# Score tasks and a probability task placed between the key blocks of the weighted sums, and three exponents ahead of ScalarE's copy of the heads

## The reference

```python
x = x + attn(layernorm(x))       # q, k, v = x @ Wq, x @ Wk, x @ Wv; s = (q * scale) @ k^T, causal
                                 # p = softmax(s); o = p @ v; attn = o @ Wo + bo
x = x + moe(layernorm(x))        # top 2 of 8 experts by softmax of x @ gate_w^T
                                 # relu(x @ w1[e] + b1[e]) @ w2[e] + b2[e], weighted by the probabilities
```

## Time and profile before

| | us |
|---|---|
| median of 3 runs | 533.49 (533.24 to 535.54) |
| span of the profiled execution | 527.7 |
| TensorE busy | 469.7 (89%) |
| VectorE busy | 413.1 (78%) |
| ScalarE busy | 358.9 (68%) |
| GpSimd busy | 286.6 (54%) |

### The profile page before, as it was taken

How to read it: one execution, slowest core, us unless ns; L and a number is a source line. 1 busy time by engine, 2 the same in 40 slices (tenths; PEclk the granted TensorE clock), 3 DMA queues, 4 the chain that set the end, 5 groups by cost and what they waited for, 6 DMA issues and landing times.

```text
span 527.7 us, 14330 instructions
## 1 busy us (share of the span) xinstructions
PE 469.7 (89%) x4121; PEld 328.0 (62%) x4121; DVE 413.1 (78%) x1519; ACT 358.9 (68%) x782; POOL 286.6 (54%) x579
## 2 busy tenths in 40 slices
PE   3788999999999999999999999989788789999981
PEld 1545656556555545546555545459688679999980
DVE  6898878988988888888888897875556555557875
ACT  7576877777867867876866857875456457777750
POOL 5603544535755766657657565725456555545542
PEclk9879999999999999999999999999999899999997
DMA  7434232132233233233333326722222322235653
GB/s 225 134 93 129 56 118 91 56 118 88 67 120 108 70 108 110 76 101 97 102 95 98 106 76 175 209 65 63 56 63 69 85 77 74 71 79 180 182 172 101
DMA packets 49454, 54.92 MB, mean 104 GB/s; under 512 B 6564, under 2 KB 41554, under 8 KB 49377
## 3 DMA queue, kind: packets, MB, share of 16 engines
q1 hardware_dynamic: 44736, 45.18, 29.5%
q0 software_dynamic: 4320, 8.47, 4.7%
q10 hardware_dynamic: 320, 0.36, 0.2%
HBM read 34.96 MB, written 17.90 MB: 100 GB/s over the span
## 4 chain that ended last, share of the span: by engine, by line
PE 50%; DVE 28%; ACT 7%; issue 7%; DMA 4%; another core or an unknown queue 3%; ACTq 1%; SPq 0%; POOL 0%; DVEq 0%; POOLq 0%
PE psO L1035 12%; DVE psS L1349 10%; PE psT L1197 7%; DVE maxs L1352 7%; PE psS L998 7%; PE psM L1208 5%; PE psO L1208 5%; PE psT L1011 3%; PE psS L1197 2%; ACT PT L811 2%; DMA xs_t<-sorted_x 2%; PE psS L1187 2%; DVE maxs L1349 1%; DVE xn L1278 1%
## 5 line engine op out<-in xcount | busy, mean ns | idle before, releaser
L811 ACT ACTIVATE PT<-psT 128x512 f32<-128x512 f32 x320 | 172.5, 594 | 67.6 <-PE psO L1035 45.0
L1349 DVE CUSTOM_DVE_ANT_0 psS<-mask_row,psS 128x512 f32<-128x512 bf16 (+1 forms) x232 | 142.8, 624 | 33.6 <-PE psS L998 29.3
L998 PE MATMUL psS<-Ks,Qs 96*128 96x128 bf16 (+3 forms) x512 | 132.9, 308 | 9.5 <-DVE maxs L1352 7.3
L598 POOL TENSOR_SCALAR_AFFINE_SELECT PT<-PT 128x512 f32<-128x512 f32 x124 | 76.8, 635 | 96.0 <-ACT PT L811 94.8
L1011 PE MATMUL psT<-Qs,Ks 108*128 108x384 bf16 (+3 forms) x512 | 109.9, 299 | 4.2 <-ACT PT L811 3.0
L695 POOL DMA_INDIRECT token_y<-Qs,y_row x71 | 70.8, 997 | 74.6 <-DVE Qs L1750 39.0
L998 PEld LDWEIGHTS psS<-Ks,Qs 96*128 96x128 bf16 x512 | 50.4, 99 | 53.5 <-DVE maxs L1352 26.4
L629 POOL DMA_INDIRECT sorted_x<-xn,place x64 | 64.3, 1005 | 27.6 <-issue 16.5
L1352 DVE TENSOR_REDUCE maxs<-psS 128x2 f32<-128x512 f32 (+3 forms) x120 | 75.7, 669 | 1.8 <-PE psS L1001 1.4
L1035 PE MATMUL psO<-PT,Vs 128*32 128x512 f32 (+3 forms) x1024 | 75.8, 436 | 0.3 <-DVE x_all L1375 0.3
L1011 PEld LDWEIGHTS psT<-Qs,Ks 108*128 108x128 bf16 x512 | 43.5, 97 | 32.8 <-ACT PT L811 12.9
(11 more groups left out here) (260 smaller groups left out, 741.1 us busy)
## 6 DMA issues: line engine op xcount, KB each, us to landing
Qs<-q_parts SPq DMA_DIRECT2D x96, 96.0 KB
Ks<-k_parts SPq DMA_DIRECT2D x95, 96.0 KB
xs_t<-sorted_x SPq DMA_DIRECT2D x71, 65.0 KB
w_sb<-in_L_ffn_w SPq DMA_DIRECT2D x16, 256.0 KB
k_parts<-kparts SPq DMA_DIRECT2D x8, 384.0 KB, 2.6
q_parts<-qparts SPq DMA_DIRECT2D x8, 384.0 KB, 3.6
x_all<-in_L_attn_x SPq DMA_DIRECT2D x8, 256.0 KB, 4.7
v_all<-token_y SPq DMA_DIRECT2D x4, 512.0 KB, 4.4
```

The source lines that it names most:

```text
L598: pool.affine_select(out=square, in_=square, compare_op=ALU.is_ge, fill=0.0, base=0, pattern=[[0, GH], [1, P]], channel_multiplier=-1).the ...
L811: act.activation(PT[:, n * T:(n + 1) * T], psT[:, bank, :], ACT.Exp).then_inc(prob_done[bank], 1)
L998: last = pe.matmul(psS[:, bank, c0:c0 + n], Qs[0:QK_ROWS, g, h, j * P:n], Ks[0:QK_ROWS, g, h, 0:n], start=True, stop=alone)
L1349: dve.tensor_tensor_reduce(src, mask_row[:, (CH - 1 - j) * P:], src, 1.0, NEG, ALU.add, ALU.max, maxs[:, par, j, h:h + 1]).then_inc(scores ...
```

## The change

On TensorE the four key blocks of the weighted sums no longer stand together. Score task 3 and probability task 2 stand between block 0 and block 1, score task 4 between block 3 and block 2, and `turn_shift` moves behind block 2. No instruction is added or removed. On ScalarE the exponent of probability task 2 moves from behind the copies of the heads and of the maxima to in front of them.

```diff
@@ ScalarE, step
                 exps(s, 0)
                 exps(s, 1)
+                exps(s, 2)
                 if not (first and g == 0):
                     copy_heads(s - 1, (g + 3) % GROUPS)
...
                 for n in range(2, NPROB):
-                    exps(s, n)
+                    if n > 2:
+                        exps(s, n)
@@ TensorE, step
-                weighed(*KEY_BLOCKS)
-
-                if nxt:
-                    turn_shift(s + 1, b + (g + 1) // GROUPS, (g + 1) % GROUPS)
+                weighed(KEY_BLOCKS[0])
                 sc(3)
                 if before:
                     probs(s, b, g, 2)
-                sc(4, 5)
+                weighed(*KEY_BLOCKS[1:3])
+                sc(4)
+                weighed(KEY_BLOCKS[3])
+                if nxt:
+                    turn_shift(s + 1, b + (g + 1) // GROUPS, (g + 1) % GROUPS)
+                sc(5)
                 probs(s, b, g, 3)
```

## The result

The changed kernel takes **547.36 us** (median of 4 runs, 546.71 to 547.92) against 533.8 us for the kernel before (4 runs on the same chip, 533.24 to 535.54): 1.0264 times as long, interval 1.0235 to 1.0293. The prediction was 540.3 with a range up to 546. The direction was right, the size half of what came.

A forecast was written before the change was run, and what follows sets the result against it. TensorE was taken as the fuller engine, VectorE also near its limit mid-attention. Early steps 3.4, five batch entries 3.2 and last steps 0.2 gave 6.8 us on 533.5: 540.3 us, range 529 to 546.

The forecast's parts named there:

- The bound: Attention steps: TensorE is the fuller engine, busy 42.1 of 43 us early and 37.9 of 40 in the middle.
- The border: TensorE, where narrow and full weights meet: 0.10 us each, four more borders, 0.40 us a step.
- The handover: Block 2 to ScalarE's copy to `turn_heads`: loses its cover, 0.2 us wait; with borders, score task 6 0.62 later.
- The copy of the maxima: ScalarE, behind the copy of the heads: done at 4.49 us after the sums' start, just hidden behind `turn_heads`.
- The exponent in front of the copy: ScalarE's third exponent: ends by 2.8 us, before the copy can begin at 3.43, so it costs nothing.
- VectorE's hole: VectorE's 1.16 us wait, outside the chain: filling it keeps 0.1; rival that it pays: 526 us, chance 0.17.
- how much later score task 6 comes: TensorE, per step: 0.62 us early; in the middle 0.24 (g = 1), 4.11 to 4.55 (g = 2), 0.3 (g = 3), 0.62 (g = 0).
- Where waits take it up: TensorE's waits for VectorE: five early steps pay 0.3 us; middle g = 3 pays nothing, g = 0 and 2 pay 0.2.
- The handover hit by scatters: Rival: GpSimd's scatters delay the copy with g = 0 and 2, 5 us more, 545 us; 0.13 shared with dearer borders.
- The last steps: The last three attention steps: hardly any score tasks, 0.2 us in all.
- The base: The 6.8 us, reckoned on a span of 527.7, was added to the median of 533.5 us.

The follow-up runs named there:

- the pair with extra matmuls: Kernel before plus two unread 16-column matmuls per step between key blocks: 128-column weights 521.61 us (1.0292), 32-column weights 508.97 us (1.0029).
- first and second set: Two sets of follow-up runs, each on one chip together with the kernel before, which took 507.39 and 507.19 us there.
- Putting a task back as cover: Changed kernel with score task 6 ahead of `turn_heads`: 519.47 us, 1.025 times the kernel before.
- a late copy alone, with no border: Kernel before with only ScalarE's new order, the third exponent in front of the copies, and TensorE's old order: 526.0 us, 1.0374 times before.
- the second set: Changed kernel run again, beside parts of the change, on a chip where the kernel before takes 507.19 us: 524.04 us, 1.0337 times before.
- the third set: Kernel before (533.37 us) with edits to ScalarE's and GpSimd's lists; with the scatter issued in the next step, 536.87 us, 1.0066 times before.

## Why the prediction had the sign right and the size wrong

**The bound: right for three groups of four.** TensorE was the fuller engine, and 68% of the chain after runs through it. Steps with g = 0 hang in part on VectorE, as below.

**The border: right, a little small.** Forecast 0.10 each, 0.40 a step. The changed kernel's step shows 0.13 + 0.09 + 0.14 + 0.10 = 0.46, and the pair with extra matmuls 0.44. The pair also shows that it hangs on the width of the weights, not on cutting the run. The Trainium skill, TensorEngine Tiling (Array Packing), section Tiling Modes, says that a change of the mode "drains the TensorE". These runs agree that a change of the width costs, 0.11 us a border; whether that time is a drain, no run here shows. Measured as that pair's difference, the borders are worth 12.7 us, against a loss of 16.9 for the whole change (first and second set; the kernel before takes 507 us in both).

**The handover: right, a little small.** Copy 3.43, `turn_heads` 4.08, score task 6 at 4.55 were forecast; 3.51, 4.16 and 4.65 came. Of that 0.1 the borders' excess is 0.06. The copy of the maxima, which was forecast as just hidden, ends at 4.57 (64.86), and `turn_heads` to score task 6 is 0.49 instead of 0.44. Putting a task back as cover gives 4.6 of the 16.9 us. With the borders' 12.7 that makes 17.3, but the parts don't simply add: a late copy alone, with no border, costs 18.6, and TensorE's order with ScalarE's old one 20.9. The two costs are each shown; how the 16.9 divide between them is not. The exponent in front of the copy cost nothing there, as forecast. It even saves some 4 us beside TensorE's new order (+20.9 without it, +16.9 with it, each against its own set; 1.6 of that lies in one step, the 26th).

**VectorE's hole was slack: right but for g = 0.** Task 6 at 5.25 forecast, 5.36 measured, and the kernel that moves score task 3 alone loses 5.7 us, near half of what four borders cost. Only in the steps with g = 0 did the filled hole pay: there VectorE's task 6 stands at 5.36 to 5.50 in the changed kernel (steps 8 to 20) and at 5.61 to 5.65 before.

**The step that failed: how much later score task 6 comes.** The table compares each step with the same step before. "Later" is score task 6, summed over the steps; "longer" is the step itself, summed likewise; us.

| steps | later, forecast | later, measured | longer, forecast | longer, measured |
|---|---|---|---|---|
| 1 to 8 | 4.96 | 6.12 | 3.4 | 4.92 |
| 9 to 24, g = 1 | 0.96 | 1.47 | 0.96 | 1.45 |
| 9 to 24, g = 2 | 1.76 | 2.15 | 0.8 | 0.91 |
| 9 to 24, g = 3 | 1.2 | 3.21 | 0 | 2.53 |
| 9 to 24, g = 0 | 2.48 | 3.43 | 0.8 | 1.98 |
| 25 to 28 | 1.6 | 2.17 | 0.64 | 0.43 |
| together | 13.0 | 18.6 | 6.6 | 12.2 |

The last two columns are 5.6 us apart, and so are the first two. The sum of what waits take up, later less longer, was right: 6.4 forecast, 6.3 measured, partly by luck, as the next paragraph says. What was too small is the lateness. In the first eight steps it is 0.72 or 0.73 with g = 2 and 0, and 0.80 with g = 1 and 3, for the 0.62 forecast. The borders' 0.06 and the 0.05 of the copy of the maxima are in all of them, and with g = 1 and 3 the product of q or k between `turn_heads` and score task 6 takes 0.94 instead of 0.86. The largest part is g = 3 in the middle: 0.3 forecast, 0.71 to 0.84 measured, since the copy of the heads stands there at 3.83 to 3.88 instead of 3.43; on the chip of the second set, where it stands at 3.51, score task 6 comes at 5.59, which would be 0.40 to 0.49.

**Where waits take it up: half wrong.** The forecast "in the other five TensorE already waits about 0.3 late in the step for VectorE, and pays 0.3" held in full only with g = 0: the first eight steps paid 0.78, 0.73, 0.80, 0.43, 0.60, 0.50, 0.80 and 0.28, four of them more than the full 0.62 (what waits took up of the lateness is 0.30 and 0.45 with g = 0, 0.20 and 0.23 in steps 5 and 6, nothing in the others). For g = 3 it said "met by the waits before 236.13 (0.47): nothing", and of 0.71 to 0.84 only 0.14 to 0.20 were met. With g = 0, 0.4 was forecast as met in the middle, and 0.44, 0.45 and 0.44 were in steps 12, 16 and 20. The pair with extra matmuls says why such a wait is no slack by itself: TensorE waits for a bank that VectorE frees, but VectorE began that stretch of work late because it had itself waited for TensorE's scores of the same step. A delay at the front of the step shifts both, and the wait between them stays as long as it was (25.8 us in both kernels), with g = 0 too. Where score task 3 comes early, as in the changed kernel and in the one that moves it alone, VectorE has a head start, and the steps with g = 0 do take up some 0.3 to 0.45. So the forecast had g = 0 right for a reason that it didn't give.

**The handover hit by scatters: it happened, and yet scatters made the loss smaller.** The copy is at 3.83 to 3.88 in steps with g = 3 and 3.60 to 3.66 with g = 0 in the middle batch entries, while the chip of the second set has 3.51 there, with steps of 10.60 instead of 10.95 (g = 3) and 10.64 instead of 10.77 (g = 0). Steps 9 to 28 take 205.2 us there and 207.5 here: 2.3 us, not the 5 of the rival, and with g = 3 and 0 where it had named 0 and 2. That the scatter does it in the changed kernel is taken over from the third set, not shown: in step 15 one is issued 2.30 us after the sums' start and the copy comes at 3.87, while on the second chip one is issued at 2.31 and the copy comes at 3.51. In the kernel before, the copies with g = 1 (3.2) and g = 3 (2.8) were held up as well. An estimate of what that cost: the kernel with narrow extra matmuls, on a 507 us chip, takes 196.0 us for steps 9 to 28, and its first eight are 0.06 each longer than those of before, so before would take about 194.8 there, against 200.2 here. By that the middle steps lose about 10.4 us where scatters hardly disturb, and 7.3 here. That fits the second set's 16.9 against the 13.6 of the prediction's own pair, so on a chip of the second set the forecast would have missed by more.

**The last steps: unforeseen, and in part open.** Forecast 0.2, measured 3.7 (25.8 us before and 29.5 after, from step 29 to the experts' first transpose). On the second chip the changed kernel takes 25.9 for the same stretch, so the 3.7 is nothing that the new order brings each time. Step 30 has 1.7 of it (8.94 us, before 7.26), with waits of TensorE of 0.57 and 1.13 us, at the full clock; their cause is open. Step 31 has 2.0 (8.01, before 6.01). From 350 to 356 us TensorE was busy 5.14 of 6 us, in the next two 0.82; then it was granted 0.50, which is 1.2 GHz instead of 2.4, from about 358.2 to 361.6, and block 0 of that step's sums took 1.93 us instead of 1.06. Before, the same place of the program kept 1.00, and so did the second chip. So about 2 us go with the clock. No run isolates why it fell.

**The base.** The sum was added to the median, though it was made from an execution some 4 us faster. That partly hid the miss: 17.9 us of span against 6.8 forecast, but 13.6 between the medians. Of the 17.9, 2.6 lie ahead of the first sums and about 2 in the last steps, both in stretches where this execution was granted a lower clock.

## What to carry to other kernels

Before cutting a run of matmuls with narrow weights, count the borders: each cut makes two, they cost about 0.1 us each here, and in the pair that differed by them alone nearly all of it reached the end. Look also at what lies between the run's last matmul and whoever reads its result, since work put ahead of that matmul is taken from the cover behind it. Work out how much later the task comes for each kind of step, and not for one: the miss was a lateness taken from one step, where others had a product or a transfer more in the way. And don't credit a wait between two engines as slack before you have seen that the engine waited for wouldn't start later too; two kernels that differ by a known delay, compared wait by wait, show it directly.

## What the hardware showed beyond that

- A 16-column matmul between 32-column ones costs almost nothing if its weights are 32 columns wide (the sums' 2.18 us become 2.24 with two of them), and 0.25 us each with 128 columns.
- A scatter issued by GpSimd holds up a handover between TensorE and ScalarE: 3.20 instead of 2.43 us for the copy, and back to 2.43 once the scatter moved. Its size differs by chip: the changed kernel has the copy at 3.83 to 3.88 in middle steps with g = 3 on one chip, and at 3.51 on another.
- The same program takes 533 us in two of the four sets of runs and 507 in the two others. Little of that lies in the attention: from the first sums to those of step 31 it is 294.1 us before on a 533 us chip, and 290.1 with the narrow extra matmuls on a 507 us chip. From the experts' first transpose to the end it is 176.4 and 157.9. Why is open.
